# Moving the PSUM copy of the transposed normalised rows from VectorE to ScalarE in the last of four graph layers

## What is computed

```python
m = embs @ map_w.T + map_b
sem = m.reshape(b, s, h, dk).transpose(0, 2, 1, 3)
n = sem / norm                                   # norm of each head's 32 numbers
cos = einsum('bhsd,bhtd->bhst', n, n) * (~sm)
cos_adj = (cos > THRESHOLD)
q, k = (m @ q_w.T + q_b), (m @ k_w.T + k_b)      # split into heads
p_attn = softmax(where(sm, NEG, q k^T / sqrt(dk))) * keep
adj = cos_adj * p_attn
out = relu((adj @ (embs @ gcn_map_w.T + gcn_map_b)) @ gcn_W.T / (adj.sum(-1) + 1.0))
```

## Time and profile before

| | us |
|---|---|
| runs | 2172.36, 2172.86, 2173.91 (median 2172.86) |
| profiled execution, span from first to last instruction | 2171.3 |
| fourth layer, first to last nT copy | 1710.1 to 2155.6 |
| TensorE / VectorE / ScalarE / GpSimd busy over the span | 2089.0 / 1494.9 / 1002.0 / 504.2 |

### The profile page before, as it was taken

How to read it: one execution, slowest core, us unless ns; L and a number is a source line. 1 busy time by engine, 2 the same in 40 slices (tenths; PEclk the granted TensorE clock), 3 DMA queues, 4 the chain that set the end, 5 groups by cost and what they waited for, 6 DMA issues and landing times. The chain is left out here.

```text
span 2171.3 us, 52286 instructions
## 1 busy us (share of the span) xinstructions
PE 2089.0 (96%) x18300; PEld 1881.0 (87%) x18300; DVE 1494.9 (69%) x3312; ACT 1002.0 (46%) x2057; POOL 504.2 (23%) x562
## 2 busy tenths in 40 slices
PE   7999999799999889999999999999999899999997
PEld 6888888699999789999999999999998778777786
DVE  6877878677777545555555555555554799999997
ACT  5666666454555322222222222222222476667665
POOL 3222222222222011111111110111111444444442
PEclk9999999999999899999999999999999999999999
DMA  3222222333222201111001001111110121122111
GB/s 90 80 71 63 74 68 65 118 113 84 81 82 86 68 21 31 31 30 30 30 30 30 25 20 30 30 30 30 30 30 20 42 61 51 53 59 59 55 49 45
DMA packets 149370, 113.31 MB, mean 52 GB/s; under 512 B 42944, under 2 KB 148800, under 8 KB 149312
## 3 DMA queue, kind: packets, MB, share of 16 engines
q1 hardware_dynamic: 149312, 112.52, 18.1%
HBM read 78.93 MB, written 33.55 MB: 52 GB/s over the span
## 5 line engine op out<-in xcount | busy, mean ns | idle before, releaser
L273 POOL TENSOR_TENSOR ln_rstd<-ln_var_eps,minus_half 128x2 f32<-128x2 f32 x128 | 90.9, 710 | 1106.2 <-DVE ln_var_eps L266 1106.2
L1615 ACT ACTIVATE l_cat_hi<-banks 128x512 fp32r<-128x512 f32 x128 | 76.5, 597 | 260.4 <-PE banks L1788 260.4
L161 PE MATMUL banks<-ln_hT_hi,square_w_hi 128*128 128x256 f32 x512 | 154.8, 302 | 5.0 <-DVE square_w_lo L614 3.2
L290 ACT ACTIVATE ln_h<-ln_x,ln_shift,ln_rstd 128x256 f32<-128x256 f32 x256 | 139.4, 592 | 32.0 <-DVE ln_shift L280 23.3
L161 PE MATMUL banks<-ln_hT_hi,l_g_w_hi 128*128 128x256 f32 x512 | 149.3, 292 | 4.9 <-POOL l_a_bd L1568 4.9
L163 PE MATMUL banks<-ln_hT_hi,square_w_lo 128*128 128x256 f32 x512 | 146.0, 285 | 0.0
L162 PE MATMUL banks<-ln_hT_lo,square_w_hi 128*128 128x256 f32 x512 | 145.7, 285 | 0.0
L161 PE MATMUL banks<-l_cat_hi,l_aw_hi 128*128 128x256 f32 x512 | 144.2, 282 | 1.4 <-DVE l_cat_lo L1675 1.4
L163 PE MATMUL banks<-l_cat_hi,l_aw_lo 128*128 128x256 f32 x512 | 144.1, 281 | 0.0
L162 PE MATMUL banks<-l_cat_lo,l_aw_hi 128*128 128x256 f32 x512 | 143.8, 281 | 0.0
L163 PE MATMUL banks<-ln_hT_hi,l_g_w_lo 128*128 128x256 f32 x512 | 143.1, 279 | 0.0
(11 more groups left out here) (227 smaller groups left out, 6910.8 us busy)
## 6 DMA issues: line engine op xcount, KB each, us to landing
hidden<-y SPq DMA_DIRECT2D x96, 256.0 KB, 2.2
ln_x<-hidden SPq DMA_DIRECT2D x96, 256.0 KB, 2.8
x_res<-hidden SPq DMA_DIRECT2D x96, 256.0 KB, 2.9
ln_x<-x SPq DMA_DIRECT2D x32, 256.0 KB, 2.9
x_res<-x SPq DMA_DIRECT2D x32, 256.0 KB, 3.0
out<-y SPq DMA_DIRECT2D x32, 256.0 KB, 2.2
l_adj_u<-adj SPq DMA_DIRECT2D x96, 16.0 KB, 2.4
l_stage_attnT<-L_attnT SPq DMA_DIRECT2D x4, 256.0 KB, 3.3
```

What stands on the lines that cost most here:

```text
L161: nc.tensor.matmul(out, lhs(lh), rhs(rh), start=start, stop=False, skip_group_check=True)
L273: self.nc.gpsimd.tensor_tensor(self.rstd[:, g.slot], self.var_eps[:, g.slot], self.core.minus_half[:, 0:PAIRS], ALU.pow).then_inc(self.rst ...
L290: last = self.nc.scalar.activation(self.h[:, u, p, :], self.x[:, u, p, :], ACT.Relu, bias=self.shift[:, u, p:p + 1], scale=self.rstd[:, u, ...
L1615: nc.scalar.activation(cat_hi[:, h * KC:(h + 1) * KC], halves(B_HP[h]), ACT.Relu).then_inc(cat_hi_ready.sem, 1)
```

## The change

In `step` of the fourth layer VectorE no longer copies nT between its second `shifted` and the layer norm's `bn_aggr`. ScalarE makes the same copy (all 128 partitions, 512 numbers each, from PSUM bank 0 to `nT`) between q and `exponentials(1)`. VectorE waited for ScalarE's reading of the old `nT` (`n_bd_ready`); ScalarE waits for VectorE's (`n_bd_dve_ready`).

```diff
@@ scalar, step @@
                     last.then_inc(q_ready.sem, 1)
                 if c2.exists(groups):
+                    after(act, nT_in_psum, c2)
+                    after(act, cos_in_psum, c2.back(2))
+                    after(act, n_bd_dve_ready, c2.back(2))
+                    nc.scalar.activation(nT[:, c2.slot], ps[:, B_HT, :].rearrange("p (c t) -> p c t", c=KC),
+                                         ACT.Copy).then_inc(nT_ready.sem, 1)
                     exponentials(1)
                     after(act, nT_ready, c2)
@@ vector, step @@
                 if c2.exists(groups):
                     softmax_shift(1)
-                    after(dve, nT_in_psum, c2)
-                    after(dve, cos_in_psum, c2.back(2))
-                    after(dve, n_bd_ready, c2.back(2))
-                    nc.vector.tensor_copy(nT[:, c2.slot], ps[:, B_HT, :].rearrange("p (c t) -> p c t", c=KC)).then_inc(
-                        nT_ready.sem, 1)
                 if gn is not None:
                     ln.statistics(dve, gn, first=False)
```

## The result

| | before | after |
|---|---|---|
| median, 9 runs each | 2172.86 us | 2179.81 us |
| lowest to highest | 2171.58 to 2177.01 | 2176.40 to 2183.13 |
| span of the profiled execution | 2171.3 | 2179.8 |

The ratio is 1.0026 with a 95% interval of 1.0017 to 1.0036, so the change costs about 5.6 us (3.7 to 7.8); the two medians are 6.95 us apart. The forecast was 2179.2 us, slower.

The account below looks back on a forecast made before the run. Two equally long loops, VectorE's and one through TensorE and ScalarE, bound the kernel; ScalarE's grows by 0.21 us in each of 30 groups, so 2172.9 + 6.3 = 2179.2 us, range 2170 to 2187.

Parts of the forecast that it names:

- The two loops: Fourth layer: VectorE's loop and one through TensorE and ScalarE are equally long, about 14.4 us per step.
- the second loop: scores(0) to q on TensorE, q to linkedT on ScalarE, then the next scores(0): 14.36 and 14.43 us.
- the gap before prob: ScalarE's gap behind q, where prob waited for VectorE's shifted; the moved copy was to fill it.
- ScalarE's delay: n_bd and all behind it on ScalarE come 0.29 and 0.14 us later, a mean of 0.21 per group.
- the covered part: 0.06 us of one step's delay, hidden because linkedT there waited for TensorE's transposes, which would now be earlier.
- The sum: Over the layer's 30 groups that count, 30 x 0.21 = 6.3 us slower, giving 2179.2 us.
- VectorE's relief: VectorE's loop shortens by 0.10 us per step and not 0.60, since m must wait for TensorE's product M.
- New waits: VectorE waits some 0.5 us at m; TensorE idles some 0.3 before scores(0), about 0.46 before the transposes of linked.
- The occupancy rule: Rival: VectorE alone bounds and ScalarE's slack takes the copy; 18 us faster, about 2155; chance of this large gain 0.07.
- rival 3: ScalarE's copy starts only when q is done: 0.52 us per group, 2188.5 us; chance 0.10 including what lies between.

Follow-up runs that it names:

- experiment 5: Kernel before without the third of ScalarE's three n_bd instructions; ratio to before 0.9994, step 14.394 us against 14.395.
- experiment 2: Kernel before with VectorE's copy of nT taken out and put nowhere; ratio to before 1.0010, step 14.361 us.
- experiment 6: Changed kernel without the third of ScalarE's three n_bd instructions; ratio to the kernel before 0.9966, step 14.189 us.
- experiment 4: Changed kernel with ScalarE's copy behind the second exponential and not ahead of it; ratio to the kernel before 1.0096, step 14.986 us.
- experiment 3: Kernel before plus a same-size copy of a constant tile on ScalarE between q and the second exponential; ratio to before 1.0041, step 14.612 us.
- experiment 7: Changed kernel with VectorE's first sum over prob moved ahead of bn_aggr; ratio to the kernel before 1.0021, step 14.568 us.
- last attempt of experiment 8: Changed kernel, one more n_bd quarter moved from ScalarE to VectorE, first sum over prob ahead of m, m_sq's sum behind first linked; ratio to before 1.0014.

## Why the prediction was right, point by point

- **The two loops.** Read from 0.05 us between linkedT and scores(0) and from equal lengths. Shown: relief of one engine alone changes the step by 0.034 (VectorE) or 0.001 (ScalarE), load on ScalarE alone lengthens it by 0.217. Two parts of the reading don't stand: the 0.05 doesn't tell the loops apart (experiment 5), and before the change the second loop ran to prob over VectorE's shifted and not over q (experiment 2). The sum was right even so, since it counted the gap before prob and let the copy fill it.
- **ScalarE's delay**, predicted 0.29 and 0.14, mean 0.215. Measured: n_bd at 1.73 behind q and not 1.77, the step longer by 0.175. The copy started at 0.73 (0.74 predicted); the exponential followed 0.47 to 0.48 behind it, where the row of the second layer had 0.50, and n_bd another 0.52 behind that, where I had 0.53 from a step in which it may have waited for nT. These hundredths are the difference of 0.04. Step by step it also fits: n_bd moved from 1.49 and 1.57 to 1.73, which with the covered part taken off is 0.24 and 0.11.
- **The sum.** 30 x 0.175 = 5.3 in place of 6.3. The medians differ by 6.95 us, the ratio says 5.6; forecast 6.3. The layer itself is only 4.5 and 4.3 us longer in the two profiles, because 1.1 and 1.0 us come back behind the last q, where the prediction put nothing. That the median lies 0.6 us from the forecast is therefore partly luck: a cost read about 2 us too high met other time of about that size outside the changed layer.
- **VectorE's relief**, predicted 0.10 per step, was too small by half: 0.21 (experiment 6). Experiment 2 agrees: there linkedT starts 0.95 after the transposes start, so VectorE's loop has 0.18 to spare in a step of 14.36. A likely cause is in the rows: from the start of y to the start of the sum over prob VectorE took 1.53 before (1971.81 to 1973.34) and 1.40 in experiment 6 (1984.28 to 1985.68), as the last section shows; I didn't test it by itself. It didn't matter for the time, since ScalarE's loop bound. If it hadn't, this term would have been wrong by a factor of two.
- **New waits.** VectorE at m 0.43 (predicted some 0.5), TensorE at scores(0) 0.31 (some 0.3), at linked 0.38 (0.46), VectorE busy 90.9 in 100 (about 90).
- **The occupancy rule** of the Trainium skill (Perfetto Trace Analysis, Identifying the Most-Contended Engine) would have had the change gain. Here it didn't hold: the busier engine of the two was relieved, and the less busy one held the step. Experiment 2 shows that the fault isn't in where the work went, since with the work gone altogether the gain was 0.03 per step.
- **The copy doesn't overlap** (rival 3) would have given 0.52 per step. Experiment 4 shows a price of that size (0.59) when the copy stands where there is no gap and its reader is next.

## What to carry to other kernels

An engine with a third of its time free can still be the bound, if its idle time lies ahead of the wait that starts its run and not inside it. Before moving work, follow the loop from one step's start through the engine to the next step's start, and look whether the receiving engine has a gap between those two points; if it hasn't, the move costs its spacing there, less what gap it fills. That an instruction starts 0.05 us behind another engine's shows only that the other one is on the way; what that one waited for shows whose loop it is. Where two loops are equally long, a gain needs both to be shortened, and each thing moved must be looked up again for what stands behind it on its new engine.

## What the runs showed of the hardware that I hadn't expected

- **VectorE's y or shift takes 0.7 to 0.85 us longer when it starts while GpSimd makes m_sq.** The timeline of the kernel before, and then that of the changed one:

```profile
1971.81 0.69 DVE L1284 SCALAR_TENSOR_TENSOR y<-l_t,x_res 128x512 f32<-128x512 f32 x1
...
1972.26 1.15 POOL L1109 TENSOR_TENSOR l_m_sq<-l_m 128x512 f32<-128x512 f32 x1
...
1972.42 1.00 DVE L280 SCALAR_TENSOR_TENSOR ln_shift<-ln_mean_var,ln_rstd 128x2 f32<-128x2 f32 x1
```

```profile
1979.07 1.09 POOL L1109 TENSOR_TENSOR l_m_sq<-l_m 128x512 f32<-128x512 f32 x1
```

  Before, the shift of 128x2 numbers runs beside m_sq and takes 1.00 us, and y takes 0.69. In the changed kernel y begins at 1979.30, beside m_sq, and takes 1.41, and the shift behind it 0.15. I didn't vary this by itself, but the order differs among the kernels. In ten of the fourteen profiles one of the two starts beside m_sq in the steady steps, and it is the long one each time: the shift in the kernel before and in experiments 3, 5 and 7, y in both profiles of the changed kernel and in experiments 2, 4 and 6. In the last attempt of experiment 8 it is the shift in 26 steps and y in the other two. The sum over prob that starts beside m_sq keeps its 0.67, and the row maximum and shifted beside GpSimd's product for n (also 128x512) keep 0.68 to 0.69. Why it meets these two and not the others isn't shown. A VectorE instruction's duration in one order isn't safe in another.
- **A PSUM copy of 128x512 on ScalarE costs 0.47 to 0.50 us of its time in a run of instructions, though its row says 0.60**, and a reader of its result that comes next on the same engine starts 0.61 behind its start (experiment 4). With the exponential between the two, the reader starts 0.52 behind the exponential, as it did without the copy (0.53).
- **GpSimd took 1.75 to 2.04 us in the steady steps for a copy of 32x512** that takes VectorE 0.42 and ScalarE 0.63.
